# Fused cross-attention block on one core: V of step 0 in two other PSUM banks, weight splits redistributed, normalisation placed later, last step in halves

## The reference

```python
h = _layernorm(x, gamma, beta)
Q = (h @ Wq).reshape(B, NQ, N_HEADS, HEAD_DIM)
K = (context @ Wk).reshape(B, NC, N_HEADS, HEAD_DIM)
V = (context @ Wv).reshape(B, NC, N_HEADS, HEAD_DIM)
attn = jnp.einsum('bihd,bjhd->bhij', Q, K)
attn = jax.nn.softmax(attn, axis=-1) * scale
vals = jnp.einsum('bhij,bjhd->bihd', attn, V).reshape(B, NQ, INNER)
out = vals @ Wo + bo
return x + out
```

## Time and profile before

| | us |
|---|---|
| median of three runs | 374.44 |
| lowest, highest | 373.33, 374.57 |
| profiled execution, device time | 374.68 |
| span of the profiled execution | 372.9 |

### The profile page before, as it was taken

One profiled execution on the slowest core, in us unless ns is written; L12 is line 12 of the kernel. 1 busy time (PEld: TensorE's weight loads), 2 busy tenths in 40 slices (PEclk: granted clock), 3 DMA queues, 4 the chain that ended last, 5 costly groups with the idle time before them and its releaser, 6 DMA issues.

```text
span 372.9 us, 8902 instructions
## 1 busy us (share of the span) xinstructions
PE 356.7 (96%) x3122; PEld 308.4 (83%) x3122; DVE 245.6 (66%) x534; ACT 252.6 (68%) x757; POOL 161.1 (43%) x314
## 2 busy tenths in 40 slices
PE   5896999999999999999999999999999999999984
PEld 4776888988888888888889888889888888988863
DVE  5877576675668656595656866676665956566552
ACT  5776866677766667776667777666776766677761
POOL 6437772445532373332624445324733335333330
PEclk9998999999999999999999999999999999999999
DMA  6940010020002000020000200010000000000000
GB/s 173 262 130 1 5 49 2 0 80 1 2 2 60 20 0 0 0 77 0 0 1 0 77 0 0 0 48 29 0 0 0 28 2 0 3 2 29 3 0 30
DMA packets 10135, 10.39 MB, mean 28 GB/s; under 512 B 864, under 2 KB 9056, under 8 KB 10112
## 3 DMA queue, kind: packets, MB, share of 16 engines
q1 hardware_dynamic: 9728, 9.77, 9.1%
q0 software_dynamic: 112, 0.13, 0.4%
q10 hardware_dynamic: 272, 0.20, 0.2%
HBM read 8.00 MB, written 2.10 MB: 27 GB/s over the span
## 4 chain that ended last, share of the span: by engine, by line
PE 91%; DVE 3%; ACT 3%; POOL 1%; issue 1%; POOLq 0%; DVEq 0%
PE st_ps L705 15%; PE mix_ps L642 15%; PE o_ps L693 13%; PE st_ps L623 13%; PE w_ps L672 12%; PE w_ps L661 11%; PE w_ps L724 10%; ACT prob L381 2%; PE w_ps L606 1%; PE w_ps L598 1%; DVE qk_lo L523 1%; DVE w_lo L442 1%; PE o_ps L593 1%; POOL w_lo L264 1%; DVE neg_max L510 1%
## 5 line engine op out<-in xcount | busy, mean ns | idle before, releaser
L292 POOL TENSOR_SCALAR prob<-prob,inv 128x256 f32<-128x256 f32 x256 | 121.6, 491 | 162.2 <-DVE inv L517 162.2
L381 ACT ACTIVATE prob<-st_ps,neg_max 128x256 f32<-128x256 f32 x256 | 118.6, 474 | 26.4 <-DVE neg_max L510 26.2
L510 DVE TENSOR_REDUCE neg_max<-st_ps 128x2 f32<-128x512 f32 x128 | 82.6, 684 | 35.4 <-PE st_ps L623 35.1
L425 ACT ACTIVATE prob_t<-st_ps 128x512 f32<-128x512 f32 x64 | 38.4, 599 | 49.7 <-PE st_ps L705 49.7
L575 DVE COPY prob_t<-st_ps 128x512 f32<-128x512 f32 x64 | 44.3, 692 | 37.0 <-PE st_ps L705 33.5
L642 PE MATMUL mix_ps<-prob_t,v_sb 128*64 128x256 f32 x512 | 62.3, 385 | 0.1
L705 PE MATMUL st_ps<-ident,prob 128*128 128x128 f32 x512 | 61.8, 274 | 0.0
L705 PEld LDWEIGHTS st_ps<-ident,prob 128*128 128x128 f32 x512 | 57.4, 142 | 0.1
L523 DVE TENSOR_TENSOR qk_lo<-w_ps,qk_hi 128x512 fp32r<-128x512 f32 x64 | 44.0, 688 | 17.6 <-ACT qk_hi L391 17.1
L381 ACT ACTIVATION_READ_ACCUMULATOR prob<-st_ps,neg_max 128x1 f32 x256 | 52.8, 206 | 0.0
L642 PEld LDWEIGHTS mix_ps<-prob_t,v_sb 128*64 128x64 f32 x512 | 34.0, 136 | 18.2 <-issue 0.3
(11 more groups left out here) (70 smaller groups left out, 579.5 us busy)
## 6 DMA issues: line engine op xcount, KB each, us to landing
x_in<-in_x_dram SPq DMA_DIRECT2D x8, 256.0 KB, 3.0
out_dram<-y_sb SPq DMA_DIRECT2D x8, 256.0 KB, 2.2
c_in<-in_ctx_dram SPq DMA_DIRECT2D x7, 192.0 KB, 2.9
w_raw<-in_L_xattn_Wo_dram SPq DMA_DIRECT2D x4, 256.0 KB, 7.6
w_raw<-in_L_xattn_Wk_dram SPq DMA_DIRECT2D x4, 128.0 KB, 4.8
w_raw<-in_L_xattn_Wq_dram SPq DMA_DIRECT2D x4, 128.0 KB, 3.3
w_raw<-in_L_xattn_Wv_dram SPq DMA_DIRECT2D x2, 256.0 KB, 7.0
w_raw<-in_L_xattn_Wv_dram SPq DMA_DIRECT2D x4, 128.0 KB, 6.6
```

Of the source, the lines that this page charges most:

```text
L292: last = nc.gpsimd.tensor_scalar(prob[:, e, r, :], prob[:, e, r, :], inv[:, e, r:r + 1], SCALE, ALU.mult, ALU.mult)
L381: last = nc.scalar.activation(prob[:, e, r, :], st_ps[e][:, r * ROWS:(r + 1) * ROWS], ACT.Exp, bias=neg_max[:, e, r:r + 1], accum_out=sums ...
L510: nc.vector.tensor_reduce(neg_max[:, e, :], st_ps[e][:, :].rearrange("p (r j) -> p r j", r=RT), AX, ALU.max, negate=True).then_inc(max_rea ...
```

## The change

1. PE waits apart for high and low parts (`high_ready`, `low_ready`): the high passes of a product no longer wait for the low parts. In the first Q product this also holds for `h_lo`. The third block of six warming transposes (`keep_warm`, L593) is gone.
2. In step 0 V goes to `mix_ps` and `o_ps`, both halves in a row, ahead of `turn_c`. `statistics(1)` stands between DVE's two `keys_lo` of step 0.
3. Pieces 10 to 19 are split elsewhere: the high part of 13 on DVE in step 0, 14 and 15 on ACT between Exps of step 1, 18 and 19 at the end of step 2. The low parts of 10, 11, 12, 14, 15, 17, 18 and 19 are on POOL; DVE keeps 13 and 16. 14 and 15 are ahead of POOL's scaling of step 1, 17 behind it, 18 and 19 behind that of step 2. `bias(0)` goes to step 2, the load of the output bias behind five weight parts.
4. `norm` stands behind both `keys_lo`, in front of the copies `prob_t`, in every sequence.
5. Step 32: the mix goes to two banks, `mix_hi` and `mix_lo` are made by pair, `last_output` writes rows 0 and 1 to `w1_ps` and `st_ps[0]`; `x_bias` and the sum so far are added ahead of it, and the two row halves are added and stored apart, one by SP, one by ACT.
6. The loop begins one step later; `LOAD` follows it, and the order of SP's transfers stays.

```diff
-    LOOP_FROM, LOOP_STEPS, LOOPS = 2, 2 * PER_SEQ, 3
+    LOOP_FROM, LOOP_STEPS, LOOPS = 3, 2 * PER_SEQ, 3
...
-    LO_VECTOR = (0, 4, 5, 8, 9, 10, 11, 14, 15, 16)
-    LO_POOL = (1, 2, 3, 6, 7, 12, 13, 17, 18, 19)
-    HI_LATE = {0: (10, 11), 1: (14, 15, 16)}
-    LO_VECTOR_LATE = {0: (10, 11), 1: (14, 15, 16)}
-    LO_POOL_LATE = {0: (12, 13), 1: (17, 18, 19)}
+    HI_VECTOR = (13,)
+    LO_VECTOR = (0, 4, 5, 8, 9, 13, 16)
+    LO_POOL = (1, 2, 3, 6, 7, 10, 11, 12, 14, 15, 17, 18, 19)
...
             deviation(0)
-            pool.dma_start(bo_b[:, :], b_o.partition_broadcast(P)).then_inc(bo_in, 16)
             for n in (1, 2, 3, 6, 7):
                 weight_lo(n)
+            pool.dma_start(bo_b[:, :], b_o.partition_broadcast(P)).then_inc(bo_in, 16)
...
+                if u == 1:
+                    weight_lo(14)
+                    weight_lo(15)
                 if 0 <= u < STEPS:
                     for e in range(HEADS):
                         pool.wait_ge(inv_ready, HEADS * u + e + 1)
...
-                for n in LO_POOL_LATE.get(u, ()):
+                for n in {0: (10, 11, 12), 1: (17,), 2: (18, 19)}.get(u, ()):
                     weight_lo(n)
-                if u == 1:
+                if u == 2:
 
                     pool.wait_ge(bo_in, 16)
                     bias(0)
...
                 probabilities(0)
                 if u == 1:
-                    weight_hi(13)
+                    weight_hi(14)
                 probabilities(1)
-                if 1 <= u <= STEPS:
+                if u == 1:
+                    weight_hi(15)
+                if u == STEPS:
+
+                    for a in range(BATCH):
+                        act.wait_ge(mixed, u + a)
+                        nc.scalar.activation(mix_hi[:, a, :], (mix_ps, w0_ps)[a][:, 0:ROWS],
+                                             ACT.Copy).then_inc(mix_hi_ready, 1)
...
-                if u == 1:
-                    for n in (17, 18, 19):
-                        weight_hi(n)
+                for n in {1: (17,), 2: (18, 19)}.get(u, ()):
+                    weight_hi(n)
...
+            act.wait_ge(y_ready, SEQS + 1)
+            act.dma_start(y_v[SEQS - 1, :, 1, :], y_sb[:, 1, 1, :]).then_inc(y_free[1], 16)
...
+                if u == LAST - 1:
+                    dve.wait_ge(y_part, 1)
+                    for r in range(RT):
+                        dve.wait_ge(o_added, STEPS + r)
+                        nc.vector.tensor_tensor(y_sb[:, 1, r, :], (w1_ps, st_ps[0])[r][:, 0:D],
+                                                y_sb[:, 1, r, :], ALU.add).then_inc(y_ready, 1)
...
+                if t == 0:
+                    pe.wait_ge(h_hi_first, 1)
+                    pe.wait_ge(h_second, 2)
+                elif p == 0:
+                    pe.wait_ge(h_lo_ready, DT * b + DT + turns(4))
+                for n, (w, h) in enumerate(((w_hi, h_hi), (w_lo, h_hi), (w_hi, h_lo))):
+                    if n == 1 and t in FOR_Q:
+                        low_ready(pe, FOR_Q[t])
+                    if n == 2 and t == 0:
+                        pe.wait_ge(h_lo_ready, DT)
...
+                ps = (mix_ps, o_ps)[n] if n < RT else w0_ps
...
                 if u == 0:
                     values(0, turns)
+                    values(1, turns)
```

More of the change, by code:

```diff
@@ L173, in walk, with before, high_ready, low_ready @@
                 step(u, lambda n: 0)
[L175 to L186 removed]
+        def before(n, pieces):
+            return sum(1 for piece in pieces if piece < n)
+        def high_ready(engine, n):
+            engine.wait_ge(w_hi_ready, n - before(n, HI_VECTOR))
+            if before(n, HI_VECTOR):
+                engine.wait_ge(w_hi_vector_ready, before(n, HI_VECTOR))
+        def low_ready(engine, n):
+            engine.wait_ge(w_lo_ready, before(n, LO_VECTOR))
+            engine.wait_ge(w_lo_pool_ready, before(n, LO_POOL))
+        LOAD, STATS, TURN_C, NORM, SPLIT_C, SPLIT_H, PUT = -5, -4, -4, -3, -3, -2, PER_SEQ + 1
         @block.sync
@@ L243, in _ @@
             walk(sp, step)
-            for k in range(2):
-                sp.wait_ge(y_free[k], 16 * (SEQS // 2 + 1))
+            sp.wait_ge(y_free[0], 16 * (SEQS // 2 + 1))
+            sp.wait_ge(y_free[1], 16 * (SEQS // 2 + 2))
         @block.gpsimd
@@ L540, in step @@
                     weight_lo(9)
-                b = of_seq(u, NORM, 1)
-                if b is not None:
-                    dve.wait_ge(x_turned, b + turns(2))
-                    norm(b, turns)
-                if 1 <= u <= STEPS:
+                if u == STEPS:
+                    for a in range(BATCH):
+                        dve.wait_ge(mix_hi_ready, u + a)
+                        nc.vector.tensor_tensor(mix_lo[:, a, :], (mix_ps, w0_ps)[a][:, 0:ROWS],
+                                                mix_hi[:, a, :].bitcast(fp32), ALU.subtract)\
+                            .then_inc(mix_lo_ready, 1)
+                elif 1 <= u < STEPS:
                     dve.wait_ge(mix_hi_ready, u + turns(8))
@@ L565, in step @@
                             .then_inc(h_hi_ready, 1)
+                if u == 0:
+                    statistics(1, turns)
                 keys_lo(1)
-                for n in LO_VECTOR_LATE.get(u, ()):
-                    weight_lo(n)
+                if u == 0:
+                    weight_hi(13)
+                    weight_lo(13)
+                if u == 1:
+                    weight_lo(16)
+                b = of_seq(u, NORM, 1)
+                if b is not None:
+                    dve.wait_ge(x_turned, b + turns(2))
+                    norm(b, turns)
                 if 0 <= u < STEPS:
@@ L639, in mix @@
                     p = (BATCH * w + a) % GROUP
+                    own_bank = w == STEPS - 1 and a == 1
+                    ps, first = (w0_ps, 0) if own_bank else (mix_ps, a * ROWS)
                     for j in range(RT):
@@ new lines, in keys @@
+                if t in FOR_K:
+                    high_ready(pe, FOR_K[t])
+                if p == 0:
+                    pe.wait_ge(c_lo_ready, b + 1 + turns(2))
+                passes = context_products(K0)
+                for n, (w, i, k) in enumerate(passes):
+                    if n == CT and t in FOR_K:
+                        low_ready(pe, FOR_K[t])
+                    nc.tensor.matmul((w0_ps, w1_ps)[a][:, 0:ROWS], w[:, i, cols],
+                                     c_t[:, b % 2, k, :], start=n == 0, stop=n == len(passes) - 1,
+                                     skip_group_check=True)
@@ new lines, in queries @@
+            def queries(t, a, turns):
+                b, p = divmod(t, PAIRS)
+                cols = slice(p * P, (p + 1) * P)
+                if t in FOR_Q:
+                    high_ready(pe, FOR_Q[t])
+                if t == 0:
[8 more added lines that the diff above has]
+                        pe.wait_ge(h_lo_ready, DT)
+                    for d in range(DT):
+                        last = nc.tensor.matmul((w0_ps, w1_ps)[a][:, ROWS:2 * ROWS],
+                                                w[:, Q0 + d, cols], h[:, b % 2, d, :],
+                                                start=n == 0 and d == 0,
+                                                stop=n == 2 and d == DT - 1, skip_group_check=True)
+                last.then_inc(projected, 1)
@@ L698, in output, with last_output @@
                 last.then_inc(o_added, 1)
+            def last_output():
+                for a in range(BATCH):
+                    pe.wait_ge(mix_lo_ready, STEPS + a)
+                    o, cols = divmod(PAIRS - BATCH + a, GROUP)
+                    cols = slice(cols * D, (cols + 1) * D)
+                    for r in range(RT):
+                        passes = ((mix_hi, w_hi), (mix_lo, w_hi), (mix_hi, w_lo))
+                        for n, (m, wt) in enumerate(passes):
+                            last = nc.tensor.matmul(
+                                (w1_ps, st_ps[0])[r][:, 0:D], m[:, a, r * P:(r + 1) * P],
+                                wt[:, O0 + o, cols], start=a == 0 and n == 0,
+                                stop=a == BATCH - 1 and n == 2, skip_group_check=True)
+                        if a == BATCH - 1:
+                            last.then_inc(o_added, 1)
             def turn(u, turns):
```

133 lines of the change are left out of this document (65 added, 68 removed).

## The result

| | before | after |
|---|---|---|
| median, us | 373.91 | 377.62 |
| lowest, highest | 373.33, 374.57 | 377.33, 378.2 |
| profiled execution, device time | 374.68 | 378.20 |
| its span | 372.9 | 376.3 |

The ratio is 1.0091, with a 95% interval of 1.0069 to 1.0114: the changed kernel is 0.9% slower. The prediction was 368.6, faster, with a range that ended at 371.0. It was wrong in size and in sign.

The account below looks back on a forecast made before the run. PE, busy 356.7 of 372.9 us, was taken as the bound, so only its idle or slow time could be won. Terms -4.4 + 1.5 - 1.6 - 1.4 = -5.9 gave 368.8 or 368.5; predicted 368.6, range 366.8 to 371.0.

Parts of the forecast that it names:

- E: Rival: too many PE gaps before step 0, lower clock from there into step 1, 10.2 us lost, 378.8; chance 0.03.
- F: Rival: several shares of C, D and a weak end together, no net change, 374; chance 0.04.
- C: Rival: the clock falls again in step 1 or at step 3's stall, price 1.83, 370.4; chance 0.20.
- D: Rival: step 1's ACT and POOL chain longer by two stretched POOL instructions and a late transfer, 371.0; chance 0.11.
- The head and steps 0 and 1: Start of kernel to step 2's first score product: a gain of 4.4 us (3.3 to 5.2), 1.83 of it clock.
- S0: First score product of step 0: forecast about 0.5 us earlier, near 12.3.
- S1: First score product of step 1: forecast about 0.95 us earlier than 24.13, at 23.2.
- S2: First score product of step 2: forecast at 36.3 us against 40.72, at full clock.
- The 1.83 for the clock: Step 1, output product to next scores: 1.83 us gained because PE's clock no longer falls to 0.50.
- Step 3: New stall: PE's Q product waits 1.1 us for POOL's h_lo, later transposes 0.4; loss 1.5 (0 to 2.2), once.
- Normalisation: Six steps with x_norm moved behind keys_lo: output product no longer 0.26 us longer, gain 1.6 (0.8 to 1.7).
- The end: Last step by pairs and row halves: gain 1.4 us (1.0 to 1.8), storing in two halves counted at nothing.

Follow-up runs that it names:

- e3: Changed kernel with 90 idle instructions at the head of PE's list: 372.03 us, ratio 0.9942 to the kernel before.
- e6: Changed kernel with its loop beginning at step 2 again and the high parts of 18 and 19 on ACT at the end of step 1: 367.32 us.
- e7: e6 plus h_lo of sequence 1 ahead of POOL's low parts of 18 and 19, and piece 13's high part on ACT, low part later on DVE: 366.57 us.
- e11: e7 with V of step 0 in bank w0 again, its halves apart: 368.31 us.
- e1: Kernel before with only its loop (and the loads with it) beginning one step later: 386.16 us, ratio 1.031.
- e2: Kernel before with 170 idle instructions at the head of PE's list: 391.57 us, ratio 1.0474.
- e12: Changed kernel with 30 idle instructions at the head of PE's list: 379.13 us, ratio 1.0132 to the kernel before.
- e4: Changed kernel with its loop written out, so no jumps back: 368.45 us, ratio 0.9846 to the kernel before.
- e8: e4 with the normalisation of all steps but the first back ahead of mix_lo on DVE: 370.0 us.
- e5: Kernel before with its loop written out, nothing else changed: 374.71 us, ratio 1.000.

## Why the prediction was wrong, step by step

**The step that failed is part 6, the later loop.** The front of the document lists it as a part of the change, and the working gives it one sentence, that the SP transfers have several steps of slack. That was right and beside the point. I asked what the moved boundary does to DMAs that are issued steps ahead and not what it does to PE's own instruction list; the cost of the jumps back stood at nothing, without a reason. In its place the runs show 3.5 and 6.4 us lost at the two jumps, 9.9 in all. The boundary moved PE's loop by one step, some 200 instructions, less than a packet of 260 to 280, and with that PE fetched again at each jump: 13 packets in all in the kernel before, e3, e6, e7 and e11, 31 in the changed one, e1, e2 and e12, nine more for each of two jumps.

The Trainium skill, "Runtime: NRT & Kernel Launch", section Instruction fetch mechanics, says that PE's instruction memory is 128 KiB, refilled in blocks of 16 KiB, 256 instructions, that crossing such a border is mostly hidden, and that a taken branch whose target is not in the window stalls. The size of a packet, the 260 to 280 instructions for each in e4 and the hidden fetching of the flat lists agree; 128 KiB would be eight such blocks. Its window of two pages doesn't agree: a jump back over 1552 loads and products, some six packets by the count of e4, cost nothing in the kernel before, e3, e6, e7 and e11.

With the 256 instructions that the Trainium skill gives a block, an estimate says what decides. The body, with some 120 waits and register instructions beside its 1552, is about 6.5 blocks. In the changed kernel it begins, by the place of the second gap, about 50 instructions ahead of a border, so it touches eight blocks; one step earlier it begins just behind a border and touches seven. By this count every kernel whose body touches seven kept them, and every kernel whose body touches eight did not. The count itself is argued, not measured: no run began between about 40 instructions (e3) and 170 (e2) behind a border, and none had a body of another length. What the runs show is that the place of the body in PE's list decides.

How much a jump costs is in two parts. The gaps are 3.2 us at each jump of the changed kernel (1.74 + 1.44, 1.46 + 1.72). At the second one 3.2 of the 6.4 us come from the clock: mix, K and Q at 0.50. Whether a gap brings the clock down isn't settled by its length. Behind the first gap of each of the six pairs (changed kernel, e1, e12; 1.30 to 1.74 us) the products ran at a granted clock of 1.00. Behind the second (1.44 to 2.45) it fell to about 0.50 in five of six, and stayed at 1.00 behind the one of 1.44. The single gaps of e2 (2.54 and 2.62) were followed by 0.50.

**Which rival came true?** None. E (378.8) came nearest to 377.62, and that is luck: it was a lower clock from before step 0 on, and the clock was 1.00 in 12.8 to 24.1 us. F (374) was a sum of shares of C, D and a weak end; the clock was 1.00 in 30 to 34 us, around the output product of step 1, where it had been 0.50 behind that product's start, and the end was better. The list of rivals had the same blind spot as the sum: all were waits between engines.

**The head and steps 0 and 1: -4.4, measured -4.2.** The sum held while its two halves did not. S0 came 0.49 earlier, as forecast. Transposes of probabilities began at 20.94 (I had 21.25). S1 came at 24.06 instead of 23.2: the term "late by 0.3" for DVE's parts of piece 13, taken at 1.3 to 2.0 us, was 1.21, since they took 3.0. I had priced the sharing of SBUF only for POOL, by the earlier trace rows, and here it was DVE that was stretched. The sentence of the Trainium skill that the prediction cites ("GPSIMD Engine Reference", section Key points) names the contention without saying which side pays. The rest of step 1 went as written. The output product began at 30.30 with no hole before it, 6.2 behind S1 (predicted 6.3), the scaling at 30.09 and the transposes waited for it:

```profile
30.09 4.12 POOL L305 TENSOR_SCALAR prob<-prob,inv 128x256 f32<-128x256 f32 x8
...
34.27 0.66 PE L797 MATMUL st_ps<-ident,prob 128*128 128x128 f32 x4 [0.71 <-POOL prob L305]
```

S2 was 36.44 (predicted 36.3): the scaling ended 10.15 behind S1 where I had 10.5, and of the pieces behind it I had rounded 0.4 upwards. Two errors of about 0.8 cancelled. The 1.83 for the clock rests on the profile; e2 gives 1.67 for the same stretch at full clock (6.61 - 4.94). That holds against the slower group of the kernel before only: its faster group is 1.3 us shorter at a higher mean clock, probably without this fall.

**Step 3: +1.5, measured +1.2.** The stall is where it was predicted, and e6 and e4 differ by 1.13 us for it alone. The Q product waited 0.70 for `h_lo` (predicted 1.1), and the rest came behind it, where the transposes waited for POOL's scaling, 0.46 by difference (predicted 0.4):

```profile
46.79 2.53 POOL L274 TENSOR_TENSOR w_lo<-w_raw,w_hi 128x512 fp32r<-128x512 f32 x2 [2.34 <-ACT w_hi L339]
49.28 1.41 POOL L285 TENSOR_TENSOR x_bias<-x_in,bo_b 128x256 f32<-128x256 f32 x2
50.65 1.43 POOL L319 TENSOR_TENSOR h_lo<-h_full,h_hi 128x256 fp32r<-128x256 f32 x2
...
52.13 0.50 PE L747 MATMUL w_ps<-h_hi,w_hi 128*128 128x256 f32 x2 [0.70 <-POOL h_lo L319]
```

**Normalisation: -1.6, measured -1.6** in the table and 1.55 by e8. **The end: -1.4, measured -1.9.** The products were right: from the start of the last mix to the last output product 5.05 before and 3.85 now. The sum in halves I had at 0.2 and the store in halves at nothing; together they gave 0.7: the last sum and store now need 2.8 us behind the last product instead of 3.5. The last sum of e4 takes 0.41 where one of 0.69 stood:

```profile
363.97 0.41 DVE L545 TENSOR_TENSOR y_sb<-st_ps,y_sb 128x256 f32<-128x256 f32 x1
```

**What stays open.** Why nine blocks and not eight are fetched per jump (one ahead would explain it), why the fetches leave two visible gaps in most runs and one in e2, and what of the clock's fall behind a gap is chance. Where exactly between the places that were tried the body stops fitting, and how the time goes up with longer bodies, was not tried.

## What to carry to other kernels

Where a change moves a loop's boundary or adds instructions in front of or into a loop on the busiest engine, count its instructions: whether the body is fetched anew depended here on where it begins in the list, and the cost came at every jump back, once for the gap and mostly again for the clock. The page of the profile shows it before any step is looked at: packets of the instruction queue up from 13 to 31, and waits for "issue" at the steps where the loop turns. Writing the loop out costs nothing here (e5) and takes the question away; a weight part that is moved next to another engine's is priced for both engines.

## What the runs showed of the hardware that I had not expected

- Whether a loop body of about 1670 instructions on PE (1552 and an estimate of 120) is fetched anew at each jump back depends on where it begins: 90 idle instructions at the head of the list changed 377.62 to 372.03 us, 30 changed it to 379.13, and 170 changed the kernel before from about 374.7 to 391.57, 8.1 of which are their own time.
- A jump back to code that is fetched anew costs 3.2 to 3.8 us in two gaps (e12: 1.30 + 1.88 and 1.30 + 2.45), in e2 2.5 to 2.6 in one, and in seven of the eight jumps of the changed kernel, e1, e2 and e12 about 1.3 to 3.2 us more by a lowered clock.
- An idle instruction of PE at the head of the list takes 0.073 us (first product at 7.40 behind 90 of them, at 13.21 behind 170); the first 3.8 us are hidden in the wait for the identity matrix, so that 30 cost next to nothing.
- The same wait of 2.17 us of PE in step 1 was followed by a granted clock of 0.50 in the kernel before and by 1.00 in e2, which is worth 1.67 us.
- DVE's cast from SBUF to SBUF of 128x512 took 0.42 us before POOL's subtraction began and 1.39 us when it began behind one; its subtraction took 0.69 us when it began ahead of POOL's and 1.65 when it began behind it.
